# Four row-by-row tiles in a layer's last step instead of three, and row numbers loaded by eight, in a graph network kernel

## The reference

```python
def _gine_layer(x, src, dst, edge_attr, eps, We, be, W1, b1, gamma, beta, W2, b2):
    e = edge_attr @ We + be
    m = relu(x[src] + e)
    agg = segment_sum(m, dst, num_segments=x.shape[0])
    h = ((1.0 + eps) * x + agg) @ W1 + b1
    mu, var = mean(h, axis=0), mean(square(h - mu), axis=0)
    h = relu((h - mu) * rsqrt(var + BN_EPS) * gamma + beta)
    return relu(h @ W2 + b2)

for l in range(4):
    x = _gine_layer(x, src, dst, edge_attr, eps[l], ...)
return layernorm(x_in + x)
```

## Time and profile before

| | |
|---|---|
| median of 3 runs | 1330.37 us (1326.92 to 1331.89) |
| the profiled execution | 1327.09 us, its span 1325.3 us |
[...]
| TensorE busy | 1191.3 us, 90% of the span |
| VectorE busy | 1035.2 us, 78% |
| GpSimd busy | 818.9 us, 62% (860 gathers) |
| ScalarE busy | 517.8 us, 39% |
| row-by-row DMAs of SyncE | 1536, 2 KB each |
| DMA | 261.77 MB, 198 GB/s on average |

### The profile page before, as it was taken

The page is one execution under the profiler, slowest core; times in us unless marked ns, Lnnn a source line. Parts: engine busy times, 40 slices in busy tenths (PEclk is TensorE's granted clock), DMA queues, the critical chain, the costliest instruction groups (busy, mean ns, idle before and its releaser), DMA issues.

```text
span 1325.3 us, 24747 instructions
## 1 busy us (share of the span) xinstructions
PE 1191.3 (90%) x7309; PEld 737.7 (56%) x7309; DVE 1035.2 (78%) x2108; ACT 517.8 (39%) x1130; POOL 818.9 (62%) x871
## 2 busy tenths in 40 slices
PE   3657999999897999999797999999898799999787
PEld 2633666666543566666453566665454466666453
DVE  7949789988667978877666978787766978788668
ACT  2752343434272334333273333433254333343233
POOL 0047777777417777777707777777715777777720
PEclk9578999999798999999899999999799999999899
DMA  3157777777547777777737777777746777777753
GB/s 110 62 151 214 216 216 215 217 215 217 185 124 230 215 216 216 215 215 215 244 104 224 214 216 216 216 215 216 234 143 195 215 216 215 215 216 215 226 163 120
DMA packets 93299, 261.77 MB, mean 198 GB/s; under 512 B 19497, under 2 KB 22304, under 8 KB 93162
## 3 DMA queue, kind: packets, MB, share of 16 engines
q0 software_dynamic: 68800, 225.50, 58.3%
q1 hardware_dynamic: 24362, 34.64, 8.1%
HBM read 246.93 MB, written 12.94 MB: 196 GB/s over the span
## 4 chain that ended last, share of the span: by engine, by line
POOL 43%; PE 30%; issue 14%; DVE 9%; DMA 2%; ACT 1%; POOLq 0%; ACTq 0%; DVEq 0%
POOL rows L771 43%; PE y_ps L1987 9%; PE y_ps L1864 6%; PE pair_ps L1813 5%; DVE rows L1422 2%; PE h_ps L1942 2%; DVE rows L1333 2%; PE y_ps L1998 1%; DMA rows<-node_table,src_fast 1%; ACT src_bc L840 1%; PE uT_ps L1895 1%; PE uT_ps L1902 1%; DMA node_table<-rows 1%; PE uT_ps L1888 1%; PE pair_ps L1928 1%
## 5 line engine op out<-in xcount | busy, mean ns | idle before, releaser
L771 POOL DMA_INDIRECT rows<-node_table,src_fast x860 | 816.3, 949 | 451.4 <-issue 340.9
L1422 DVE SCALAR_TENSOR_TENSOR rows<-We_ps,negw_fast,rows 128x512 f32<-128x512 f32 x860 | 593.3, 743 | 167.9 <-DMA rows<-node_table,src_fast 167.3
L948 ACT ACTIVATE rows<-y_ps 128x512 f32<-128x512 f32 x380 | 224.6, 602 | 519.9 <-PE y_ps L1864 509.6
L1864 PE MATMUL y_ps<-table_parts,src_onehot 128*128 128x512 f32 x1520 | 407.9, 416 | 11.2 <-DVE table_parts L611 8.0
L1813 PE MATMUL pair_ps<-rows,onehot 128*32 128x512 f32 x2504 | 329.7, 620 | 69.0 <-DVE rows L1422 68.5
L1864 PEld LDWEIGHTS y_ps<-table_parts,src_onehot 128*128 128x128 f32 x1520 | 273.7, 192 | 202.3 <-issue 87.4
L1813 PEld LDWEIGHTS pair_ps<-rows,onehot 128*32 128x32 f32 x2504 | 61.3, 110 | 210.2 <-issue 101.9
L1942 PEld LDWEIGHTS h_ps<-uT,W_sb 128*128 128x128 f32 x1152 | 135.5, 194 | 7.0 <-issue 4.2
L1269 DVE TENSOR_TENSOR src_onehot<-y_ps,src_bc 126x256 fp32r<-126x256 f32 x352 | 137.8, 413 | 0.0
L1942 PE MATMUL h_ps<-uT,W_sb 128*128 128x128 f32 x1152 | 136.5, 277 | 0.0
L1987 PE MATMUL y_ps<-rows,hT 128*128 128x512 f32 x288 | 124.5, 593 | 0.0
(11 more groups left out here) (239 smaller groups left out, 775.9 us busy)
## 6 DMA issues: line engine op xcount, KB each, us to landing
late_rows<-node_table SPq DMA_DIRECT2D x1536, 2.0 KB
rows<-node_table,src_fast POOLq DMA_INDIRECT x860, 3.8
node_table<-rows SPq DMA_DIRECT2D x29, 256.0 KB, 3.3
src_onehot<-near_ws SPq DMA_DIRECT2D x380, 2.0 KB
x_now<-x_pad SPq DMA_DIRECT2D x10, 512.0 KB, 7.3
W_sb<-W SPq DMA_DIRECT2D x4, 1024.0 KB, 5.5
rows<-W SPq DMA_DIRECT2D x16, 256.0 KB, 4.1
out<-rows SPq DMA_DIRECT2D x8, 256.0 KB
```

The source lines that it names most:

```text
L771: nc.gpsimd.indirect_dma_start(rows[:, slot, :], None, table[:, :], bass.IndirectOffsetOnAxis(src_fast[:, t:t + 1], 0)).then_inc(landed[q] ...
L948: nc.scalar.activation(rows[:, slot, :], y_ps[k % 2][:, :], ACT.Relu).then_inc(tile_ready, 1)
L1422: last = nc.vector.scalar_tensor_tensor(rows[:, slot, :], We_ps[:, :], negw_fast[:, t:t + 1], row, ALU.mult, ALU.max)
L1864: last = nc.tensor.matmul(y_ps[k % 2][:, :], src_onehot[:, 2 * (k % ONEHOTS) + b, :], table_parts[:, part, 2 * pair_of(k) + b, :], start=( ...
```

## The change

SyncE fetches tile 12 of each layer's last step row by row as well. It stands first among the four, and its rows go to b2_bc, the buffer of the second bias, which is free until the bias is loaded. GpSimd gathers it no more. One load of numbers fills eight registers instead of four, so a piece behind a load_w_rows has eight row DMAs.

```diff
-    ROW_TILES = [13, 14, 15]
+    ROW_TILES = [12, 13, 14, 15]
     ROW_BYTES = 4 * D
     ROW_GUARD, ROW_PIECE = 192, 32
-    AT_ONCE = 4
+    AT_ONCE = 8
@@
-        late_rows = sb("late_rows", [P, len(ROW_TILES), D])
+        late_rows = sb("late_rows", [P, len(ROW_TILES) - 1, D])
@@
+        late_tiles = [late_rows[:, m, :] for m in range(len(ROW_TILES) - 1)] + [b2_bc[:, :]]
@@ def load_rows(m, c, a):
-                    sp.dma_start(late_rows[p:p + 1, m, :].bitcast(u8),
+                    sp.dma_start(late_tiles[m][p:p + 1, :].bitcast(u8),
                                  table_bytes[:, bass.ds(place_of, ROW_BYTES)]).then_inc(rows_landed[m], 16)
@@ def messages(q, l, i):
-                        row = late_rows[:, m, :]
+                        row = late_tiles[m]
```

## The result

The changed kernel takes 1578.47 us (median of 4 runs, 1576.75 to 1580.69), the kernel before 1329.42: a ratio of 1.190, 95% interval 1.188 to 1.193. It is 19% slower. The profiled execution has a span of 1576.3 us against 1325.3, 251.0 us more. Lines from 230 on have moved down by one.

The account below looks back on a forecast made before the run. GpSimd and TensorE run nearly level, with SyncE's queue at 96% of the needed pace. The profiled 1327.1 us plus 233.9 of stall minus 36 given back makes 1525, forecast as 1528 us, range 1475 to 1591.

Parts of the forecast that it names:

- piece, per near tile: On SyncE's queue, weight rows, one load of eight numbers and eight row DMAs take 3.65 us, against a need of 2.40.
- from tile 74's weight rows to ScalarE: ScalarE takes tile 74 3.8 us after its weight rows are issued: 2.7 for the landing, 1.05 for four matmuls.
- given back: After tile 74, gathers done during the stall shorten the layer's end: 9 us per layer, 36 in all, bounds 0 and 48.
- the allowance for nothing given back: In the range's upper end, 36 us added in case the last step is bound by something unseen.
- The start and the end of the stall: TensorE's stop for weight rows begins near tile 25 to 30, with the 20 us lead gone, and ends with tile 74.
- the ceiling of 48: At each layer's end, twelve gathers saved (nine ahead, one removed, as worked out) give back at most 48 us in four layers.
- the nine in hand: At tile 74 GpSimd restarts with 9 gathers already done during the stall, worth 11 us.
- The removed gather: Tile 12 leaves GpSimd's queue in each last step: 4 x 1.25 = 5.0 us less, the most it could bring.
- The cover by the lead: Rival: with SyncE's piece at most 2.72 us, tile 74 is in time and the kernel takes 1325 us; chance 0.06.
- The dearer load: Rival: SyncE's load of eight is two loads or costs per number, 146 us more, 1674 us; chance 0.10.
- The clock: Rival: TensorE falls to the half clock during the stall, 171 us more, about 1700 us; full price 0.03.
- its signs: Profile after: line 658 every 3.5 to 3.7 us, TensorE waiting some 200 us for src_onehot's DMA, GpSimd's count at 856.

Follow-up runs that it names:

- e4: The changed kernel with the same loads of eight numbers, but only the first four rows of each piece fetched; 1323.5 us, ratio 0.998.
- e9: The changed kernel with only five row DMAs behind each near tile's weight rows, the 87 left over behind the last; 1364.0 us, ratio 1.027.
- e5: The changed kernel with two pieces of four behind each near tile instead of one of eight; 1679.9 us, ratio 1.268.
- e6: The changed kernel with sixteen numbers at once instead of eight, so 32 pieces a layer; 1785.7 us, ratio 1.348.
- e10: The kernel before (three tiles, by four) with the weight rows of near tiles 11 to 95 issued by ScalarE; 1328.2 us, ratio 1.001.
- e8: The changed kernel with the weight rows of near tiles 11 to 95 issued by ScalarE instead of SyncE; 1323.7 us, ratio 0.999.

## Why the prediction was right, and where its sum was short

The direction, the mechanism and the place were as forecast, and 1578 lies in the range of 1475 to 1591, but near its upper end. The terms, for the profiled execution:

| term | forecast | measured | difference in four layers |
|---|---|---|---|
| piece, per near tile | 3.65 us | 3.855 us | +52 us |
| from tile 74's weight rows to ScalarE | 3.8 us | 6.8, 5.3, 6.5, 5.2 us | +9 |
| given back | 36 us | 43 us | -7 |
| sum | 1525 us | 1578 us | +54, by its terms |

**The piece.** Its step failed by its size, and the stated bounds of 3.51 to 3.74 didn't hold. Two prices in it were short. The load of eight is 784 ns, not 640: 0.14 us too little. I had bounded the price of a number from above by 30 ns, with SyncE's load of four against ScalarE's load of one. That bound needs both engines' loads to lie on one line, for which I had no row: one number takes 471 ns on ScalarE, 487 on TensorE, 507 on GpSimd and 543 on VectorE. On SyncE alone, 561, 784 and 1232 ns for four, eight and sixteen numbers are 56 ns a number throughout, and that line would put one number at about 390 ns, an estimate, since no run has a SyncE load of one. The other is the row DMAs. I divided 1.23 us by four; but a group's duration ends with its last DMA and holds one gap less. Eight take 2.53 us, so four more are 1.30 us and not 1.24. 0.14 + 0.06 = 0.20 us, times 256 pieces 52 us, which is nearly the whole error. The share for the hiccups (0.06) was right: 3.855 against 3.79 in the clean stretch. That the range held in spite of this is owed to the allowance for nothing given back: without its 36 us the range would have ended at 1555.

**The start and the end of the stall.** It began in layer 1 at about 530 us, near tile 25, and ended with tile 74, both as forecast. The 3.8 us from the weight rows to ScalarE were too few, because TensorE isn't always waiting just there. It serves its fixed order:

```profile
715.31 2.04 PE L1865 MATMUL y_ps<-table_parts,src_onehot 128*128 128x512 f32 x4 [4.09 <-DMA src_onehot<-near_ws]
717.16 4.25 PE L1943 MATMUL h_ps<-uT,W_sb 128*128 128x128 f32 x32
721.34 1.92 PE L1814 MATMUL pair_ps<-rows,onehot 128*32 128x512 f32 x16
723.19 3.14 PE L1865 MATMUL y_ps<-table_parts,src_onehot 128*128 128x512 f32 x12
```

The weight rows of tile 72 are issued at 712.5 and its matmuls begin at 715.3, a landing of 2.8 us, where 2.7 were assumed. Tiles 73 and 74 then find TensorE at the block's product and at a quad's sum, 6 us.

**What was given back.** 294.4 us late at tile 75 and 251.0 at the end: 43.4 came back, between the 36 taken and the ceiling of 48. But it isn't even. By the starts of the layers it is 4.2 us in layer 0 and 12.9, 12.6 and 13.6 in the others. The stretch from the 75th near tile to the next layer's first, in layers 0 and 2, before and after (PE, PEld, DVE, ACT, POOL, clock, DMA):

```profile
280.80:406.70 125.90, 119.84 (x699) 73.24 (x699) 94.63 (x203) 54.94 (x126) 65.32 (x69) 0.92 0.62 188
889.40:1016.80 127.40, 116.78 (x616) 67.71 (x615) 91.28 (x186) 52.55 (x116) 70.27 (x74) 0.94 0.65 198
...
351.70:473.40 121.70, 115.24 (x701) 69.99 (x700) 89.64 (x194) 54.89 (x126) 60.32 (x63) 0.97 0.61 181
1092.60:1207.40 114.80, 110.59 (x615) 66.02 (x615) 85.05 (x176) 52.61 (x117) 61.39 (x64) 1.00 0.65 194
```

In layer 2 GpSimd has 64 gathers left to do, where it had 74. That is the nine in hand and the removed one, as forecast; in layers 1 and 3 it is 11 fewer, in layer 0 only 6. TensorE's waits for messages over these stretches are 3.4, 0.6, 1.4 and 0.6 us, where they were 3.4, 8.5, 7.8 and 13.0: 26.7 us less, none of it in layer 0. And TensorE's busy time for the same matmuls is 17.5 us less, at a granted clock of 0.97 to 1.00 of the full one where it had 0.92 to 0.96. The two make 44.2, the whole of what came back. The forecast had given the clock some 2 us a layer; it gave 4.4.

**The removed gather.** 5.0 us forecast as the most, 3.8 measured by itself (interval 1.5 to 6).

**The rivals.** The cover by the lead failed as worked out, with its limit at 2.72 us: 2.5 us in e4 and 2.56 in e9 are covered, 3.8 is not. The dearer load was half of a truth: it is one load, but it does cost per number, 56 ns. The clock fell in the stall, but without its full price:

```profile
473.00:720.00 247.00, 186.14 (x1041) 110.09 (x1042) 148.09 (x279) 64.77 (x125) 140.93 (x150) 0.88 0.58 166
```

This is layer 1's stretch with the weight rows of tiles 10 to 74. TensorE is busy 186 of 247 us (75%, in the other layers 77 to 79%, where 65% were forecast) and has 0.88, in the other layers 0.83 to 0.86, where it had 0.97 and 1.00. SyncE's chain hides it: e5's and e6's times follow from SyncE's pieces alone within 1%.

**What the text got wrong in its signs.** It looked for the wait under the name of the DMA of src_onehot, about 200 us. The time is there, 192 us, but only 37 under that name. Line 659 came every 3.8 us, above the 3.5 to 3.7. The 21 weight rows from tile 74 on have no piece between them, but they don't follow at 0.3 us: they take 29.9 us from 720.09 on, 23.4 of it waiting until the tile ten before is made. The other signs came: 856 gathers, 255 us more idle time of GpSimd, TensorE's share at 81%, no wait for the row loads after the last step.

## What to carry to other kernels

SyncE, which here only issues and loads numbers, has no row of busy time in the page, and while it had its lead it had no share of the chain either; without the lead it has 15%. So for each queue take the period of its repeating pattern, compare it with the period of what it feeds, and read the lead: in this case 2.31 us against 2.40 and 20 us were enough to forecast 60 us late in each layer from 1.3 us more per tile (74 were measured, for 1.5). Where urgent and patient transfers share a queue, count what stands ahead of each urgent one, not the sum of the queue; of the kernels that fetch all four tiles, sixteen at once had the least work for SyncE and was the slowest. Price an instruction by the same engine's own rows, and take a group's gaps as well as its members.

## What the runs showed of the hardware

- SyncE's load of numbers from SBUF to registers takes 561 ns for four, 784 for eight and 1232 for sixteen, 56 ns a number more. By that line some 0.34 us are fixed, an estimate. Even so, beside 2.53 us for eight row DMAs the load was never the larger part.
- A row DMA with its place in a register takes 0.33 us of SyncE from one to the next (2.53 us for eight, of which 0.23 for the last). 512 of them are 168 us of a layer of 305.
- ScalarE issued 85 DMAs a layer between its other work at no measurable cost (e10: 1.001, 0.999 to 1.002).
- In the stall TensorE was busy 75 to 79% of the time, and its mean granted clock was 0.83 to 0.88 of the full one; over the whole span it was 0.890, in the kernel before 0.951. The mean is made of stretches at 1.00 and at 0.50: in layer 1 it was 1.00 from 546 to 557 us, 0.50 from 558 to 561, and 1.00 again from 562 to 568. The 16 matmuls of a quad's sum took 3.20 us from 558.59 on, most of it at 0.50, and 1.92 from 721.34 on, where it was 1.00. With nothing added for the clock, the sums from SyncE's pieces gave 1687 and 1780 us for e5 and e6, and 1679.9 and 1785.7 were measured.
- The 132 us of idle time booked as issue belong to weight rows that came late: in e8, where ScalarE issues them, no wait ahead of the near tiles' matmuls is booked as issue, and of 202.0 us of idle time there 12.0 are left.
